# Second attention layer: the softmax bound moved from a selector matmul into free rows of the queries

## The chip, the cores and the metric
The kernel runs on one core of a Trainium2 chip. The metric is the device time of one execution in microseconds; lower is better. Engines: TensorE (PE, with its weight loads shown as PEld), VectorE (DVE), ScalarE (ACT), GpSimd (POOL) and SyncE (SP), which issues the DMAs here.

## What is computed
`x` is 32 images of 16 x 16 tokens with 256 channels. Each of two layers normalizes (group norm) and adds an attention of 16 heads of 16 channels. The first layer is windowed cosine attention. The second, which the change touches, attends over all 256 tokens of an image, heads 0 to 7 looking back and heads 8 to 15 looking ahead:

```python
def _masked_attention(xf, Wq, Wk, Wv, lookahead):
    q, k, v = (jnp.einsum('bnd,hed->bhne', xf, W) for W in (Wq, Wk, Wv))
    s = jnp.einsum('bhqe,bhke->bhqk', q, k) * scale
    mask = i[:, None] <= i[None, :] if lookahead else i[:, None] >= i[None, :]
    s = jnp.where(mask, s, jnp.finfo(s.dtype).min)
    return jnp.einsum('bhqk,bhke->bhqe', jax.nn.softmax(s, axis=-1), v)
```

The heads are concatenated, multiplied by `Wo` and added to the layer's input. (The snippet shortens the reference's three projections to one line.)

## The kernel before
Layer 1 of the code (`layer1`) is the second layer. An image has two channel tiles `o` of 128 channels, 8 heads each: tile 0 looks back, tile 1 ahead. A tile has four row groups `r` of 32 partitions (`own_rows(r)`), each with two heads `e` of 16 channels. A head can't be addressed alone, as a matmul takes 32 rows, so the queries are kept twice, `qm[k][:, o, e, :]`: multiplied by `own`, which is 1/4 in the rows of head `e` and 0 in those of the other head. The keys `kt` are kept once, with both heads. Scores with `qm` are therefore those of one head.

The softmax needs the maximum of each query. The kernel computes the scores twice: once with queries on partitions and masked (`bound_queries` L1011 in fp32, `mask_bounds` L1022, which adds a triangle by a bf16 matmul with the identity), from which VectorE takes the maximum (`take_max` L1165) into `cm`; and once with keys on partitions (`weigh_keys` L979), one 512-column matmul for both heads. From those the maximum is taken away on TensorE: `cm` is transposed (`turn_c` L1080), ScalarE copies it negated into bf16 `ct` (`copy_c` L1140), and `lower_by_bound` L994 adds it by bf16 matmuls with the selector `pick`. ScalarE then takes the exponential (`exponent` L1113) into `weights`, GpSimd zeroes the masked part of the diagonal blocks (`mask` L1219), and TensorE multiplies with the values (`weigh` L1042), ones beside the values giving the sums.

The work of an image is cut into six bursts: WHOLE_0 and WHOLE_0B (tile 0, two row groups each, blocks with all queries), HALVES and HALVES_B (both tiles, the other blocks, 128 columns), WHOLE_1 and WHOLE_1B (tile 1). A burst weighs two row groups of image s (PSUM banks 0, 1 of `G`) while it bounds the other two of image s+1 (banks 2, 3). Below, W0, W0B, H, HB, W1, W1B stand for the bursts and R(burst) for its maximum on VectorE.

`pipeline` runs the stages of every engine in an order written out by hand, each with a lag: lag 1 means that in step s the stage works on image s+1. TensorE's order before is W0, q/k projection of tile 1 (L1056), W0B, turn_c(1), weigh(1) of image s-1, H, value projection (L1068), HB, q/k projection of tile 0, W1, output projection of image s-2 (L1090), W1B, turn_c(0), weigh(0). ScalarE copies the weighed values out (`copy_outputs` L1127, into `ots`), queries and keys of tile 0 (L1120, L1122) and the values (L1134). VectorE copies queries and keys of tile 1 (L1171, L1173), takes four reciprocals of the sums (L1184), normalizes (L1195), divides (L1189) and adds the residual (L1178). SP regroups `ots` through DRAM in eight stores (L947), once both tiles' outputs are copied, fetches them when all eight have landed (L955) and stores results (L961). The next copy into `ots` waits for the eight stores.

Waits are semaphore counts: a burst's bounds wait for `max_done` of the burst before, its weights for `exp_done`; HALVES also wait for `qk_out[1]` and `c_out[1]`, WHOLE_0 for `qk_out[0]` and `c_out[0]`. `A[0]`, `A[1]`, `A[2]` and `E` are further PSUM tiles of 512 columns. `stack` holds queries and keys of two images.

Of the kernel before, what the change touches and what calls it, by code (L numbers as in the profile page):

```python
# [23 lines left out]
BF16 = mybir.dt.bfloat16  # L24
I32 = mybir.dt.int32
ALU = mybir.AluOpType
# [33 lines left out]
class Image:  # L60
# [6 lines left out]
    def plus(self, n):  # L67
        return Image(self.pair, self.offset + n)

# [738 lines left out]
def layer1(nc, ctx, images, out, given, scratch, X, stats2, probs, xh, stack, ident, gavg, A, G, E):  # L808
# [13 lines left out]
    ct = [sb(f"ct1{o}", [P, TOKENS], BF16) for o in range(CT)]  # L822
# [5 lines left out]
    own = sb("own", [P, 2])  # L828
    at_row = sb("at_row", [P, 2])
    pick = sb("pick", [P, 2, P], BF16)  # L830
    n_stat = images * CT
    weights = probs[1]

    flat = [stack[k][:, :, :, :].rearrange("p z h t -> p (z h t)").bitcast(F32) for k in range(2)]
    qm = [flat[k][:, 0:CT * 2 * TOKENS].rearrange("p (o e t) -> p o e t", o=CT, e=2) for k in range(2)]
    kt = [flat[k][:, CT * 2 * TOKENS:CT * 3 * TOKENS].rearrange("p (o t) -> p o t", o=CT) for k in range(2)]
# [14 lines left out]
    with nc.Block() as block:  # L851
# [7 lines left out]
        def _(dve):  # L859
# [7 lines left out]
            slots = ident[:, :].rearrange("p (r x) -> p x r", x=COL)  # L867
            nc.vector.reduce_sum(own[:, :], parity, AX_XY).then_inc(made, 1)
            nc.vector.reduce_sum(at_row[:, :], slots[:, 0:2, :], AX_X).then_inc(made, 1)
            dve.wait_ge(made, 2)  # L870
            nc.vector.tensor_scalar(own[:, :], own[:, :], DIM ** -0.5, None, ALU.mult).then_inc(made, 1)
            nc.vector.tensor_copy(pick[:, :, :], at_row[:, :].unsqueeze(2).to_broadcast([P, 2, P])).then_inc(made, 1)
# [55 lines left out]
    QK_OPS = (3, 2)  # L928
# [7 lines left out]
    with nc.Block() as block:  # L936
# [33 lines left out]
        def _(pe):  # L970
            def weigh_keys(i, b):

                if b is HALVES:
                    wait(pe, qk_out[1], i.count(QK_OPS[1]))
                wait(pe, exp_done, i.count(ALL, b.at) if b.at else i.plus(-1).count(ALL))
                for o in b.tiles:
                    for bank, r in enumerate(b.weigh_rows):
                        at = bank * 512 + b.column(o, 0)
                        nc.tensor.matmul(G[:, at:at + 2 * b.size].rearrange("p (e q) -> p e q", e=2),  # L979
                                         kt[i.k][own_rows(r), o, b.keys_of(o) * P:(b.keys_of(o) + 1) * P],  # L980
                                         qm[i.k][own_rows(r), o, :, b.queries(o)], start=(o == b.tiles[0]), stop=False,
                                         skip_group_check=True)

            def lower_by_bound(i, b):

                if b is WHOLE_0:
                    wait(pe, c_out[0], i.count(1))
                if b is HALVES:
                    wait(pe, c_out[1], i.count(1))
                for o in b.tiles:  # L990
                    for e in range(2):
                        for bank, r in enumerate(b.weigh_rows):
                            at = bank * 512 + b.column(o, e)
                            last = nc.tensor.matmul(G[:, at:at + b.size], pick[own_rows(r), e, :],  # L994
                                                    ct[o][own_rows(r), b.queries(o)], start=False, stop=True,
                                                    skip_group_check=True)
                            if e == 1 and o == b.tiles[-1]:
                                last.then_inc(s_ready, 1)

            def bound_queries(i, b):  # L1000

                if b is WHOLE_0:
                    wait(pe, qk_out[0], i.count(QK_OPS[0]))
                if b is HALVES:
                    wait(pe, qk_out[1], i.count(QK_OPS[1]))
# [42 lines left out]
            def project_qk(i, o):  # L1048

                wait(pe, xh_done, i.count(CT))  # L1050
                if o == 0:
                    wait(pe, ot_out[1], i.plus(-3).count(1))
# [236 lines left out]
```

## Time and profile before

| | us |
|---|---|
| median of 3 runs | 1286.02 (1282.92 to 1295.72) |
| profiled execution | 1287.98 |
| its span | 1286.3 |
| TensorE busy in the span | 1194.4 (93%) |
| VectorE busy | 897.7 (70%) |
| ScalarE busy | 610.9 (47%) |
| GpSimd busy | 207.4 (16%) |
| VectorE copy of k, L1173, mean | 0.415 |
| ScalarE copy of outputs, L1127, mean | 0.597 |
| fetch, L955, issue to landing, median | 2.9 |

The first layer ends near 575 us, the second fills the rest. Times in rows are microseconds from the span's start. PE is the matmul's streaming and PEld its weight load; the two overlap, and matmuls on different row groups overlap too, so the distance from one stage's first load to the next stage's first load is the way to read a stage's length. An fp32 matmul appears as two pairs of load and matmul.

### The profile page before, as it was taken

To read this page: it belongs to the slowest core of one execution; us is meant where nothing else is said; L and a number is where in the kernel's file an instruction comes from. 1 tells how busy PE (TensorE), PEld (TensorE's weight loads), DVE (VectorE), ACT (ScalarE), POOL (GpSimd) and SP (SyncE) were. 2 spreads that over 40 slices of the span, in tenths; PEclk is the share of its full clock that TensorE was granted. 3 is DMA by queue.
4 is the path that set the end of the run, shared out by engine and by line. 5 is a ranking of instruction groups with operands and counts; after the bars stand their busy time and mean duration, and the time that the engine had idled before them with its cause. 6 is when DMAs were issued, how large, how long until landed. Compare 5 with 4: busy or idle time off the path is not lost.

```text
span 1286.3 us, 50697 instructions
## 1 busy us (share of the span) xinstructions
PE 1194.4 (93%) x21404; PEld 864.1 (67%) x21404; DVE 897.7 (70%) x1591; ACT 610.9 (47%) x1019; POOL 207.4 (16%) x271
## 2 busy tenths in 40 slices
PE   6789999999999999958999999999999999999983
PEld 2567777777677677736677776767777777767652
DVE  1488898798888888645576666767666666767643
ACT  2355565555555555512444444444444444445430
POOL 0001111111111111121222212212222212222120
PEclk9699999999999999989999999999999999999987
DMA  2000000000000000010232423333232323333233
GB/s 80 13 20 20 20 17 17 20 16 25 12 24 16 18 12 3 5 38 1 34 65 64 79 48 74 52 70 57 65 58 66 75 51 76 51 71 56 67 58 74
DMA packets 304632, 54.35 MB, mean 42 GB/s; under 512 B 270724, under 2 KB 303766, under 8 KB 304534
## 3 DMA queue, kind: packets, MB, share of 16 engines
q1 hardware_dynamic: 303480, 52.75, 19.9%
q8 instruction: 83, 1.36, 0.4%
q10 hardware_dynamic: 1056, 0.13, 0.1%
q14 instruction: 13, 0.11, 0.0%
HBM read 27.56 MB, written 25.17 MB: 41 GB/s over the span
## 4 chain that ended last, share of the span: by engine, by line
PE 45%; DVE 5%; issue 3%; ACT 1%; DMA 1%; SPq 0%; POOL 0%; POOLq 0%; DVEq 0%
PE psG L979 8%; PE psA L1042 7%; PE psG L1011 6%; PE psA L1056 5%; PE psG L1022 5%; PE psE L1090 5%; PE psA L1068 4%; DVE of L1189 3%; PE psG L994 2%; DVE sums L1184 2%; PE psE L1080 1%; ACT probs L1113 0%; SPq L947 0%; DVE cm L1165 0%; DMA scratch_heads<-ots 0%
## 5 line engine op out<-in xcount | busy, mean ns | idle before, releaser
L1165 DVE TENSOR_REDUCE cm<-psG 128x4 f32<-128x1024 f32 (+1 forms) x192 | 235.2, 1225 | 174.5 <-PE psG L1022 174.3
L1113 ACT ACTIVATE probs<-psG 128x1024 f32<-128x1024 f32 x192 | 196.5, 1023 | 240.5 <-PE psG L994 240.5
L1219 POOL TENSOR_SCALAR_AFFINE_SELECT probs<-probs 128x1024 f32<-128x1024 f32 x128 | 139.1, 1098 | 551.0 <-ACT probs L1113 551.0
L979 PE MATMUL psG<-stack 32*128 32x512 f32 (+1 forms) x1024 | 219.2, 525 | 6.3 <-ACT probs L1113 6.3
L1011 PE MATMUL psG<-stack 32*128 32x256 f32 (+1 forms) x2048 | 219.2, 341 | 4.1 <-DVE cm L1165 2.7
L1011 PEld LDWEIGHTS psG<-stack 32*128 32x128 f32 x2048 | 149.6, 185 | 10.8 <-DVE cm L1165 3.4
L764 POOL TENSOR_TENSOR X<-X,probs 128x96 f32 (+5 forms) x128 | 62.0, 515 | 499.2 <-ACT probs L529 499.2
L443 PE MATMUL psA<-probs,xh 128*128 128x512 f32 x256 | 130.5, 637 | 9.3 <-ACT xh L562 5.3
L1056 PE MATMUL psA<-xh,wqk 128*128 128x256 f32 x512 | 122.6, 383 | 5.7 <-DVE xh L1195 5.7
L979 PEld LDWEIGHTS psG<-stack 32*128 32x128 f32 x1024 | 82.8, 185 | 61.6 <-issue 54.3
L1184 DVE RECIPROCAL sums<-sums 128x128 f32<-128x128 f32 x128 | 115.7, 929 | 12.0 <-DMA sums<-scratch_heads 12.0
L1056 PEld LDWEIGHTS psA<-xh,wqk 128*128 128x128 f32 x512 | 93.3, 192 | 17.4 <-DVE xh L1195 6.4
L1042 PE MATMUL psA<-probs,va 128*32 128x256 f32 (+1 forms) x2048 | 97.8, 332 | 0.9 <-POOL probs L1219 0.9
L522 ACT ACTIVATE probs<-psG 128x1024 f32<-128x1024 f32 x64 | 62.0, 1021 | 76.1 <-PE psG L346 76.1
L634 DVE TENSOR_TENSOR probs<-probs,ebias 128x1024 f32<-128x1024 f32 x64 | 77.9, 1219 | 14.6 <-ACT probs L522 14.5
L1090 PE MATMUL psE<-of,wo 128*128 128x256 f32 x256 | 67.0, 407 | 21.7 <-DVE of L1189 20.5
L707 DVE TENSOR_REDUCE cm<-psG 128x16 f32<-128x1024 f32 x64 | 75.4, 1219 | 14.8 <-PE psG L370 13.9
L1042 PEld LDWEIGHTS psA<-probs,va 128*32 128x32 f32 x2048 | 57.8, 110 | 34.5 <-issue 11.7
L506 ACT ACTIVATE probs<-psA 128x512 f32<-128x512 f32 x64 | 38.2, 597 | 87.1 <-PE psA L443 83.0
L443 PEld LDWEIGHTS psA<-probs,xh 128*128 128x128 f32 x256 | 45.6, 198 | 45.6 <-issue 33.2
L994 PE MATMUL psG<-ct,pick 32*128 32x256 bf16 (+1 forms) x1024 | 74.4, 242 | 0.0
L1090 PEld LDWEIGHTS psE<-of,wo 128*128 128x128 f32 x256 | 48.2, 198 | 36.2 <-DVE of L1189 23.2
(132 smaller groups left out, 1925.5 us busy)
## 6 DMA issues: line engine op xcount, KB each, us to landing
scratch_heads<-ots SPq DMA_DIRECT2D x256, 64.0 KB, 3.6
X<-in_xr SPq DMA_DIRECT2D x32, 256.0 KB, 2.8
raw<-scratch_heads SPq DMA_DIRECT2D x32, 256.0 KB, 2.7
sums<-scratch_heads SPq DMA_DIRECT2D x32, 256.0 KB, 3.0
out<-X SPq DMA_DIRECT2D x32, 256.0 KB, 2.9
probs<-in_wqk SPq DMA_DIRECT2D x1, 512.0 KB, 4.0
wv<-in_wv SPq DMA_DIRECT2D x2, 256.0 KB, 4.2
wqk<-in_wqk SPq DMA_DIRECT2D x1, 512.0 KB, 4.0
```

Source lines behind the costliest of these rows:

```text
L443: last = nc.tensor.matmul(A[t][:], xh[i.k][:, c, t * P:(t + 1) * P], wqk[:, c, :], start=(c == 0), stop=(c == CT - 1))
L634: nc.vector.tensor_tensor(both, both, bias.unsqueeze(2).to_broadcast([P, 4, WINDOWS, WTOK]), ALU.mult).then_inc(biased, 1)
L979: nc.tensor.matmul(G[:, at:at + 2 * b.size].rearrange("p (e q) -> p e q", e=2), kt[i.k][own_rows(r), o, b.keys_of(o) * P:(b.keys_of(o) + 1 ...
L994: last = nc.tensor.matmul(G[:, at:at + b.size], pick[own_rows(r), e, :], ct[o][own_rows(r), b.queries(o)], start=False, stop=True, skip_gr ...
L1011: nc.tensor.matmul(G[:, at:at + b.size], qm[i.k][own_rows(r), o, e, b.queries_of(o) * P:(b.queries_of(o) + 1) * P], kt[i.k][own_rows(r), o ...
L1042: last = nc.tensor.matmul(A[0 if o else 2][COL * c:COL * (c + 1), to:to + b.size], va[i.k][:, b.keys_of(o), TILE_HEADS * o + 2 * r + e, :] ...
L1056: last = nc.tensor.matmul(A[o][:, n * TOKENS:(n + 1) * TOKENS], wqk[:, c, n * CH + o * P:n * CH + (o + 1) * P], xh[i.k][:, c, :], start=(c ...
L1090: last = nc.tensor.matmul(E[:, o * TOKENS:(o + 1) * TOKENS], wo[:, f, o * P:(o + 1) * P], of[:, f, :], start=(f == 0), stop=(f == CT - 1))
L1113: nc.scalar.activation(weights[:, b.weights_at:b.weights_at + 1024], G[:, 0:1024], ACT.Exp).then_inc(exp_done, 1)
L1165: nc.vector.reduce_max(slots, scores, AX_X).then_inc(max_done, 1)
L1184: nc.vector.reciprocal(piece, piece).then_inc(r_done, 1)
L1219: nc.gpsimd.affine_select(out=diagonal, in_=diagonal, compare_op=ALU.is_ge, fill=0.0, base=0, pattern=[[0, QUADS], [0, 2], [sign, P]], cha ...
```

## The change
The bound is no longer added by matmuls of its own. The masked queries of head `e` have 16 rows that are zero, those of the other head. The transposed bound of head `e` is now laid there: `take_max` writes it to the first channel of the other head's rows (the bounds' bank column is `1 - e`), and VectorE adds the negated, transposed `cm` to `qm` in place (`fold_bound`, two `scalar_tensor_tensor` for each tile, masked by `lift`). The keys are kept per head, `km[k][:, o, e, :]`: masked by `own`, with a row of ones (`at_row` as the bias of a ScalarE `Identity`) that meets the bound. One fp32 matmul then gives scores less bound. So `lower_by_bound`, `pick`, `ct` and `copy_c` go; each 512-column weighing matmul becomes two of 256 columns (256 becomes two of 128), with a key tile of its own; the four groups' matmuls are interleaved; all k copies go to ScalarE (four for an image) and only the q copy of tile 1 stays on VectorE. `weights` uses both `probs` buffers in turn. The orders change: turn_c(1) moves ahead of the q/k projection of tile 1, the value projection ahead of H, weigh(1) behind H, and turn_c(0), now into `A[1]`, ahead of the output projection.

```diff
-            def weigh_keys(i, b): ...
-            def lower_by_bound(i, b): ...
-            def bound_queries(i, b): ...
+            def burst(j, b):
+                i = j.plus(-1)
+                weighs, bounds = i.exists(), j.among(images)
+                if weighs:
+                    if b is WHOLE_0:
+                        wait(pe, c_out[0], i.count(FOLDS))
+                    wait(pe, exp_done, i.count(ALL, b.at) if b.at else i.plus(-1).count(ALL))
+                if bounds:
+                    if b is WHOLE_0:
+                        wait(pe, qk_out[0], j.count(QK_OPS[0]))
+                    wait(pe, max_done, j.count(ALL, b.at) if b.at else j.plus(-1).count(ALL))
                 for o in b.tiles:
+                    if b is HALVES and o == 1:
+                        if weighs:
+                            wait(pe, c_out[1], i.count(FOLDS))
+                        if bounds:
+                            wait(pe, qk_out[1], j.count(QK_OPS[1]))
                     for e in range(2):
                         for bank, r in enumerate(b.weigh_rows):
+                            if weighs:
+                                at = bank * 512 + b.column(o, e)
+                                last = nc.tensor.matmul(G[:, at:at + b.size],
+                                                        km[i.k][own_rows(r), o, e, b.keys_of(o) * P:(b.keys_of(o) + 1) * P],
+                                                        qm[i.k][own_rows(r), o, e, b.queries(o)],
+                                                        start=(e == 0 and o == b.tiles[0]), stop=True, skip_group_check=True)
                         for bank, r in enumerate(b.bound_rows):
+                            if bounds:
+                                at = (2 + bank) * 512 + b.column(o, 1 - e)
+                                nc.tensor.matmul(G[:, at:at + b.size],
+                                                 qm[j.k][own_rows(r), o, e, b.queries_of(o) * P:(b.queries_of(o) + 1) * P],
+                                                 km[j.k][own_rows(r), o, e, b.keys(o)],
+                                                 start=(e == 0 and o == b.tiles[0]), stop=False, skip_group_check=True)
+                if bounds:
+                    mask_bounds(b)
...
+            pipeline(pe, images, [B(WHOLE_0), (lambda i: turn_c(i, 1), 0), (lambda i: project_qk(i, 1), 1),
+                                  B(WHOLE_0B), (project_v, 1),
+                                  B(HALVES), (lambda i: weigh(i, 1), -1),
+                                  B(HALVES_B), (lambda i: project_qk(i, 0), 2),
+                                  B(WHOLE_1), (lambda i: turn_c(i, 0), 1), (output, -2),
+                                  B(WHOLE_1B), (lambda i: weigh(i, 0), 0)], LAGS)
...
+            def copy_k(i, o):
+                if o:
+                    wait(act, qk_out[1], i.count(QK_OPS[1], 1))
+                for e in range(2):
+                    nc.scalar.activation(km[i.k][:, o, e, :], A[o][:, TOKENS:2 * TOKENS], ACT.Identity,
+                                         bias=at_row[:, 1 - e:2 - e], scale=own[:, e:e + 1]).then_inc(qk_out[o], 1)
...
+            pipeline(act, images, [(lambda i: copy_outputs(i, 0), -1), X_(WHOLE_0), (lambda i: copy_k(i, 1), 1), X_(WHOLE_0B),
+                                   X_(HALVES), (lambda i: copy_outputs(i, 1), -1), (copy_v, 1), X_(HALVES_B), (copy_q, 2),
+                                   X_(WHOLE_1), (lambda i: copy_k(i, 0), 2), X_(WHOLE_1B)], LAGS)
...
+            def fold_bound(i, o):
+                wait(dve, c_turned[o], i.count(1))
+                for e in range(2):
+                    q = qm[i.k][:, o, e, :]
+                    nc.vector.scalar_tensor_tensor(out=q, in0=(E if o else A[1])[:, 0:TOKENS], scalar=lift[:, 1 - e:2 - e], in1=q,
+                                                   op0=ALU.mult, op1=ALU.add).then_inc(c_out[o], 1)
...
+            pipeline(dve, images, [R(WHOLE_0), (lambda i: fold_bound(i, 1), 0), (copy_q, 1), R(WHOLE_0B), I_(0), (normalize, 2),
+                                   R(HALVES), I_(1), I_(2), R(HALVES_B), I_(3), (divide, -2), R(WHOLE_1),
+                                   (lambda i: fold_bound(i, 0), 1), (residual, -2), R(WHOLE_1B)], LAGS)
```

## Rows read from the trace of the kernel before

**Rows 1.** Busy time by stretch: stretch, its length, each engine's busy us (instructions), clock, DMA.
```profile
800.00:960.00 160.00, 158.63 (x1906) 114.27 (x1900) 109.40 (x125) 73.81 (x108) 33.97 (x32) 1.00 0.32 62
```

**Rows 2.** Loads of the output projection, 640 to 1240 us: durations, first and last start.
```profile
L1090 PEld LDWEIGHTS psE<-of,wo x232: 186/190/191, 650.7 to 1232.1; 128*128 128x128 f32 x116
```

**Rows 3.** Chain of waits, 912 to 925 us: start, length, what.
```profile
916.58 0.04 DVE cm L1165
...
917.72 0.95 DVE sums L1184
...
918.70 1.22 DVE of L1189
...
919.96 1.99 PE psE L1090 x8
```

**Rows 4.** Timeline of weight loads, whole bursts: start, length, instruction, [idle before <-releaser].
```profile
904.49 0.19 PEld L979 LDWEIGHTS psG<-stack 32*128 32x128 f32 x2 [0.20 <-issue]
904.51 0.19 PEld L1011 LDWEIGHTS psG<-stack 32*128 32x128 f32 x2
904.60 0.19 PEld L979 LDWEIGHTS psG<-stack 32*128 32x128 f32 x2
...
905.46 0.10 PEld L994 LDWEIGHTS psG<-ct,pick 32*128 32x128 bf16 x2 [0.22 <-issue]
905.77 0.11 PEld L1022 LDWEIGHTS psG<-above,identb 128*128 128x128 bf16 x2 [0.21 <-issue]
905.90 1.60 PEld L1056 LDWEIGHTS psA<-xh,wqk 128*128 128x128 f32 x8
907.82 0.19 PEld L979 LDWEIGHTS psG<-stack 32*128 32x128 f32 x2 [0.33 <-issue]
...
909.23 0.25 PEld L1080 LDWEIGHTS psE<-ident,cm 128*128 128x128 f32 x2
909.64 1.24 PEld L1042 LDWEIGHTS psA<-probs,va 128*32 128x32 f32 x32 [0.17 <-issue]
```

**Rows 5.** The same timeline, the burst of halves that follows.
```profile
911.08 0.19 PEld L979 LDWEIGHTS psG<-stack 32*128 32x128 f32 x2 [0.20 <-issue]
...
912.37 0.10 PEld L1022 LDWEIGHTS psG<-above,identb 128*128 128x128 bf16 x1
...
912.71 1.60 PEld L1068 LDWEIGHTS psA<-wv,xh 128*128 128x128 f32 x8
```

**Rows 6.** The same view where the pipeline fills: bursts that only bound.
```profile
581.20 0.73 PEld L1011 LDWEIGHTS psG<-stack 32*128 32x128 f32 x8 [0.33 <-DVE cm L1165]
582.26 0.11 PEld L1022 LDWEIGHTS psG<-above,identb 128*128 128x128 bf16 x2 [0.33 <-issue]
...
587.42 0.97 PEld L1011 LDWEIGHTS psG<-stack 32*128 32x128 f32 x16 [0.33 <-DVE cm L1165]
588.51 0.10 PEld L1022 LDWEIGHTS psG<-above,identb 128*128 128x128 bf16 x1
```

**Rows 7.** Timeline of VectorE in the same step.
```profile
906.20 1.23 DVE L1165 TENSOR_REDUCE cm<-psG 128x4 f32<-128x1024 f32 x1 [2.03 <-PE psG L1022]
908.02 0.69 DVE L1171 TENSOR_TENSOR stack<-psA,own 128x512 f32<-128x512 f32 x1 [0.59 <-PE psA L1056]
...
913.02 1.23 DVE L1165 TENSOR_REDUCE cm<-psG 128x8 f32<-128x1024 f32 x1 [0.85 <-PE psG L1022]
```

**Rows 8.** Groups by line and form, ScalarE: busy us, mean ns, idle before.
```profile
L1113 ACT ACTIVATE probs<-psG 128x1024 f32<-128x1024 f32 x192 | 196.5, 1023 | 240.5 <-PE psG L994 240.5
...
L1120 ACT ACTIVATE stack<-psA,own 128x256 f32<-128x256 f32 x64 | 26.8, 470 | 53.4 <-PE psA L1056 53.4
...
L1122 ACT ACTIVATE stack<-psA 128x256 f32<-128x256 f32 x32 | 12.3, 383 | 0.0
```

**Rows 9.** Timeline of SP's DMA issues.
```profile
911.95 7.11 SPq L947 DMA_DIRECT2D scratch_heads<-ots  x8
921.99 0.37 SPq L955 DMA_DIRECT2D raw<-scratch_heads  x1
```

More of the change, by code:

```diff
@@ L68, in plus, with exists @@
         return Image(self.pair, self.offset + n)
+    def exists(self):
+        return not isinstance(self.pair, int) or self.pair * 2 + self.offset >= 0
     def among(self, images):
@@ L970, in _ @@
         def _(pe):
[L971 to L975, printed above, removed]
-                for o in b.tiles:
[L977 to L982, printed above, removed]
@@ L1000, in bound_queries @@
[L1000 to L1005, printed above, removed]
-                wait(pe, max_done, i.count(ALL, b.at) if b.at else i.plus(-1).count(ALL))
-                for o in b.tiles:
-                    for e in range(2):
-                        for bank, r in enumerate(b.bound_rows):
-                            at = (2 + bank) * 512 + b.column(o, e)
-                            nc.tensor.matmul(G[:, at:at + b.size],
-                                             qm[i.k][own_rows(r), o, e, b.queries_of(o) * P:(b.queries_of(o) + 1) * P],
-                                             kt[i.k][own_rows(r), o, b.keys(o)], start=(e == 0 and o == b.tiles[0]), stop=False,
-                                             skip_group_check=True)
@@ L1043, in weigh @@
                                                     va[i.k][:, b.keys_of(o), TILE_HEADS * o + 2 * r + e, :],
-                                                    weights[:, at:at + b.size], start=b.whole, stop=not b.whole,
+                                                    weights[i.k][:, at:at + b.size], start=b.whole, stop=not b.whole,
                                                     tile_position=(0, COL * c), skip_group_check=True)
@@ L1052, in project_qk @@
                     wait(pe, ot_out[1], i.plus(-3).count(1))
+                else:
+                    wait(pe, c_out[0], i.plus(-1).count(FOLDS))
                 wait(pe, qk_out[o], i.plus(-1).count(QK_OPS[o]))
@@ L1086, in output @@
                 if i.plus(2).among(images):
-                    wait(pe, c_out[1], i.plus(2).count(1))
+                    wait(pe, c_out[1], i.plus(2).count(FOLDS))
                 for o in range(CT):
@@ L1094, in B @@
             def B(b):
[L1095 to L1103 removed]
+                return lambda j: burst(j, b), 1, 1
+            pipeline(pe, images, [B(WHOLE_0), (lambda i: turn_c(i, 1), 0), (lambda i: project_qk(i, 1), 1),
[4 more added lines that the diff above has]
+                                  B(WHOLE_1B), (lambda i: weigh(i, 0), 0)], LAGS)
         @block.scalar
```

82 lines of the change are left out of this document (27 added, 55 removed).

## The prediction
> **What bounds the kernel now.** I read the busy time by stretch first, then one step's weight loads in order of time, then the chain of waits, and last VectorE, ScalarE and the DMA queue in the same step. Between 800 and 960 us TensorE is busy for 158.63 of 160 us at a granted clock of 1.00 [rows 1]; VectorE is at 68% and ScalarE at 46%. So the second layer is TensorE's, and a step (one image) costs what its stages cost in TensorE's order. The output projection recurs 29 times between 650.7 and 1232.1 us; the last start belongs to the eighth load of its group, 1.44 us after the first, so the step is (1232.1 - 1.4 - 650.7)/28 = 20.71 us [rows 2].
>
> From load to load, a whole burst takes 1.41 us (904.49 to 905.90, again 907.82 to 909.23), a projection 1.92, a transposition of the bounds 0.41 (909.23 to 909.64), the weighing of values 1.44 (909.64 to 911.08) [rows 4, 5], a burst of halves 1.63 (911.08 to 912.71) [rows 5]. A step holds 4 x 1.41 + 2 x 1.63 + 2 x 0.41 + 2 x 1.44 + 4 x 1.92 (q/k twice, v, output) = 20.28 us. One wait is left: the output projection waits 0.37 us for the division, which stands in the chain behind R(HALVES_B), the fourth reciprocal and the product: 916.58 to 919.96, 3.38 us [rows 3]. Sum 20.65 against 20.71 for the mean step; I carry the 0.06 along.
>
> **The change, part by part.**
>
> *Selectors go.* In a whole burst the fp32 scores start at 904.49 and the mask's load at 905.77: 1.28 us, with the last L994 load at 905.46 in between [rows 4]. What a burst is without L994 the trace shows itself, where the pipeline fills and only bounds are computed: 581.20 to 582.26, 1.06 us; halves 587.42 to 588.51, 1.09 us, against 911.08 to 912.37, 1.29 [rows 5, 6]. These bursts have the same bound matmuls; the row groups of the weights run beside them. So L994 costs 0.22 per whole burst (I use 0.21, as all these times are rounded) and 0.20 per burst of halves, not the 0.31 that its own slot (905.46 to 905.77) suggests: part of that is the gap before a load over all rows, which stays. Saved: 4 x 0.21 + 2 x 0.20 = 1.24 us a step. PE work falls to 19.04 us, a whole burst to 1.20, halves to 1.43.
>
> *Keys per head.* Each weighing matmul of 512 columns becomes two of 256 (halves: 256 becomes 2 x 128). Columns are the same, but 4 (halves: 8) load-and-matmul pairs are added, as many as L994 gives up. Each of the four row groups then carries what a bound group carries today, and the bound groups set the length today. What can break this is only what the groups share. In the first two rounds of a whole burst four fp32 loads start within 0.02 us (904.49, 904.51) and the next round 0.11 later (904.60): 27 ns a pair [rows 4]. Halves need four pairs per 0.11 us throughout. Lower end: nothing. Upper end: 68 ns a pair, the slowest a burst shows (16 pairs in 1.09 us [rows 6]), although those pairs wait for their own group's stream. I take nothing, since the two full rounds are the nearest rows.
> The Trainium skill ("TensorE: Matmul & The Clock Gate", Back-to-back issue gap) gives about 81 ns for each pair of load and matmul at 128 columns in a real kernel, which would speak against this change. Today's halves contradict it for row groups: 24 fp32 and 8 L994 pairs stand in 1.29 us, 40 ns each [rows 5].
>
> *Bursts wait once, at their start.* Today only the bound half waits for the maximum. Now the weights, issued first, wait too. R starts 1.71 us after a whole burst (904.49 to 906.20), 1.94 after halves (911.08 to 913.02) [rows 4, 5, 7]; with L994 gone 1.50 and 1.74. It takes 1.23, and TensorE follows about 0.05 later (918.70 + 1.22 to 919.96 [rows 3]). So the next burst can't start before 2.78 (after halves 3.02) us. Two neighbours are close: W1B and W0 with only weigh(0) between, 1.20 + 1.44 = 2.64: wait 0.14; and H and HB with only weigh(1) between now, 1.43 + 1.44 = 2.87: wait 0.15.
>
> *The division.* H starts at 6.65 in the new order (W0 at 0; turn 1.20; q/k 1.61; W0B 3.53; v 4.73). R(H) runs 8.39 to 9.62, HB starts at 9.67, R(HB) at 11.41 (R(H) and two reciprocals before it take at most 916.58 to 918.70 plus 0.95, 3.07 us [rows 3], and end within 0.05 of that), and 3.38 later, 14.79, the output may start. TensorE is there at 14.63 (q/k 11.10, W1 13.02, turn 14.22): wait 0.16 instead of 0.37. W1B 16.71, weigh 17.91, then W0 at 19.49 with its wait. Step: 19.04 + 0.14 + 0.15 + 0.16 = 19.49, plus the 0.06: 19.55.
>
> *Folds on VectorE, k copies off it.* Two folds of 256 elements for each tile half. No row has this operation; above it lies a product of 512 from PSUM (0.69), below it half of that, 0.35, if nothing of it is fixed [rows 7]. I take 0.43, near the lower end and the plain copy of 256 in the table, since it too makes one pass over 256 elements: 0.86 a pair, 1.72 a step, less the copy of k, 0.42: VectorE rises by 1.3 us. fold(1) stands between R(W0) (ends 2.73) and copy_q, whose projection ends at 3.53 and reaches VectorE 0.2 later (905.90 to 908.02 is 2.12 [rows 4, 7]): it ends at 3.59, cover 0.14 us. fold(0) stands after R(W1), with 1 us to spare before R(W1B). At 0.69 each, copy_q starts 0.4 late.
>
> *k copies on ScalarE.* Four with a pointer scale and a pointer bias. A copy takes 383 ns, with a pointer scale 470 [rows 8]; a second pointer at the same price gives about 560, at no price 470. A pair is 1.0 us. ScalarE gains 4 x 0.56 and loses 0.38 + 2 x 0.38: about 1.1 us on some 9.9 a step. The one that can hurt is copy_k(1), in front of exp(W0B): copy_q 3.73 to 4.42, copy_k to 5.5, exp (1.02 [rows 8]) to 6.45; H needs it at 6.65. Cover 0.15. Without that cover each late us is a late us of the step; with slow folds (0.4 late) 0.25.
>
> *Later regroup.* weigh(1) moves behind HALVES, so ots is full later: weigh(1) ends at 9.52 (9.67 with the wait that follows it, no matter), its copy of 0.60 (table) is done about 0.74 later, 10.26, SP issues at about 10.4. Eight stores and their landing take 10.04 us (911.95 to the fetch at 921.99 [rows 9]): 20.43, which is 0.94 us into the next step. Behind that wait, on ScalarE, stands the first copy of outputs, and behind it exp(W0), which W0B needs at 3.53. Copy 0.94 to 1.54, exp to 2.57: cover 0.9 us. The fetch, queued behind it on SP, lands some 3 us later (table), near 4.5, before the first reciprocal at 6.2.
>
> *Two weight buffers.* exp no longer waits for the weighing of the image before, which allows the moves above; no wait of that kind ends last today. Nothing.
>
> **The sum.** 20.71 - 19.55 = 1.16 us a step. Steps with all six bursts full: 31 of the 32 images (the last has no next image's bounds): 36.0 us. The last image's six bursts without bounds lie in a serial chain with exp and gain 0.21 each, 1.3. Fill and the last two outputs, which wait for DMA, keep their length. Profiled execution: span 1286.3, time 1288.0; 1288.0 - 37.3 = 1250.7. The median of the runs shown is 2.0 lower, so 1249.
>
> **Rivals.**
> 1. *Halves don't get shorter.* If pairs there cost 40 ns as in today's halves [rows 5], 32 pairs take 1.28 instead of about 1.09, and the 0.20 isn't won: 2 x 0.2 x 31 = 12 us, 1261. For it: the spacing of today's bursts fits. Against it: their bound groups run at their own stream's pace. The same order of loss follows from slow folds or copies (0.25 x 31 = 8, 1257).
> 2. *Slower: pairs are issue- or load-bound in halves.* Place: 32 loads and 32 matmuls of 128 columns. At 68 ns a pair the burst lasts 2.18 instead of 1.09: +2.2 a step, 1249 + 68 = 1317. The gain is gone at 53 ns, slower by 1% from 59 ns. Against it: the two rounds at 27 ns.
> By the skill's 81 ns ("TensorE: Matmul & The Clock Gate", Back-to-back issue gap) it would be 2.6 us, or 1342.
> 3. *The stores become the ring.* copy_outputs(1), stores, copy_outputs(0), exp(W0), W0B, v, H, weigh(1) form a ring with 0.9 us of slack. Each us beyond it lengthens every step by one: stores of 12 us give about 1280, from 12.5 us it is slower. For it: they start later than today in the step. Against it: they meet no more traffic than today, since fetch and store of the image still fall outside them.
> 4. *The change takes L994 away but TensorE waits the same time.* The mask's load then comes 0.2 after the bounds as now: 1286. Against it: the filling bursts [rows 6], which have exactly this sequence.
>
> **How the numbers follow.** Forecast, 1240 to 1258: 0.58. Rival 1 and its like, 1258 to 1270: 0.16. Better than 1240, if the three waits also go (0.45 x 31 = 14, 1235): 0.05. Rivals 3 (part) and 4, 1273 to 1299: 0.12. Slower (2, 3): 0.09. A measurement of this kernel tells about 1% (13 us) from no change. Faster by over 1%, below 1273: 0.80; within 1%: 0.11; slower: 0.09. Range 1238 to 1270.
>
> **What would show it.** Right: no L994, output projections 19.5 to 19.6 us apart, whole bursts 1.20 and halves 1.43 from load to next stage, waits of 0.1 to 0.2 us for VectorE's maximum before HALVES_B and WHOLE_0, folds near 0.43 us. Wrong: halves longer than 1.6 us (1, 2); ScalarE's copy of outputs waiting past 1.8 us into the step (3); TensorE waiting for exp before HALVES (copy_k chain); mask loads 1.28 after the burst's start (4).

## The result

| | before | after |
|---|---|---|
| median | 1284.47 us (1277.4 to 1295.72, 4 runs) | 1248.04 us (1242.07 to 1257.64, 4 runs) |
| ratio | 1 | 0.9729 (0.9668 to 0.9791) |
| span of the profiled execution | 1286.3 | 1244.4 |
| step of the second layer | 20.71 | 19.45 |

Forecast were 1249 us and a step of 19.55. The step first: these are the loads of the output projection in the changed kernel (durations, first and last start; L1089 here, [rows 2] before):

```profile
L1089 PEld LDWEIGHTS psE<-of,wo x232: 186/190/191, 646.0 to 1192.1; 128*128 128x128 f32 x116
```

The step is (1192.1 - 1.4 - 646.0)/28 = 19.45 us. TensorE is busy for 159.41 of 160 us at a granted clock of 1.00, where it was 158.63 [rows 1]; VectorE went from 109.4 to 129.4, ScalarE from 73.8 to 86.0:

```profile
800.00:960.00 160.00, 159.41 (x1996) 114.88 (x1996) 129.44 (x158) 85.99 (x125) 35.84 (x34) 1.00 0.36 67
```

Timeline of the weight loads of one step after (start, length, instruction, idle before; L998 weighs, L1007 bounds, L1020 masks), to be held against [rows 4, 5]:

```profile
882.48 0.11 PEld L1020 LDWEIGHTS psG<-below,identb 128*128 128x128 bf16 x2 [0.33 <-issue]
882.81 1.24 PEld L1040 LDWEIGHTS psA<-probs,va 128*32 128x32 f32 x32 [0.21 <-issue]
884.25 0.19 PEld L998 LDWEIGHTS psG<-stack 32*128 32x128 f32 x2 [0.20 <-DVE cm L1165]
...
885.32 0.11 PEld L1020 LDWEIGHTS psG<-above,identb 128*128 128x128 bf16 x2 [0.33 <-issue]
885.45 0.25 PEld L1079 LDWEIGHTS psE<-ident,cm 128*128 128x128 f32 x2
885.67 1.60 PEld L1056 LDWEIGHTS psA<-xh,wqk 128*128 128x128 f32 x8
887.59 0.19 PEld L998 LDWEIGHTS psG<-stack 32*128 32x128 f32 x2 [0.33 <-issue]
...
890.72 0.19 PEld L998 LDWEIGHTS psG<-stack 32*128 32x128 f32 x2 [0.33 <-DVE cm L1165]
890.74 0.19 PEld L1007 LDWEIGHTS psG<-stack 32*128 32x128 f32 x2
890.83 0.19 PEld L998 LDWEIGHTS psG<-stack 32*128 32x128 f32 x2
...
891.83 0.10 PEld L1020 LDWEIGHTS psG<-above,identb 128*128 128x128 bf16 x1
...
892.37 1.24 PEld L1040 LDWEIGHTS psA<-probs,va 128*32 128x32 f32 x32 [0.21 <-issue]
893.81 0.19 PEld L998 LDWEIGHTS psG<-stack 32*128 32x128 f32 x2 [0.20 <-DVE cm L1165]
...
898.39 0.25 PEld L1079 LDWEIGHTS psA<-ident,cm 128*128 128x128 f32 x2
898.94 1.59 PEld L1089 LDWEIGHTS psE<-of,wo 128*128 128x128 f32 x8 [0.30 <-DVE of L1196]
```

A whole burst takes 1.20 us (884.25 to 885.45) instead of 1.41. In halves the mask comes 1.11 us after the start (890.72 to 891.83) instead of 1.29, and rounds of four pairs follow 0.11 us apart. One wait is left, before the output projection, 0.33 us: the transposition takes 0.22 from 898.39, so TensorE is free at 898.61 and starts at 898.94.

Where the 41.9 us between the two profiled spans lie, from the first load of the second layer's first projection (573.5 before, 561.8 after) and the groups of output projections: first layer, untouched by the change, -11.7; fill of the second layer up to its first output projection 77.2 and 84.2, +7.0; 28 steps at -1.26, -35.3; the last three outputs -1.9. The second layer by itself gained 30.2 us. The first part is scatter: over the profiled kernels of this study, which share this first layer, the second layer began between 557.3 and 576.7 us (579.6 in the last one below, which adds matmuls between the layers). The scatter goes together with the clock: in the four profiles in which the second layer began by 562.4 us, the granted clock stayed at 1.00 from 100 to 540 us; in each of the other eight it fell to 0.50 there once or twice, for 3.4 us each, in the kernel before once (length, PE, PEld, DVE, ACT, POOL, clock, DMA):

```profile
231.60:235.00 3.40, 3.40 (x32) 3.07 (x29) 2.44 (x4) 2.10 (x3) 0.00 (x0) 0.50 0.00 0
```

TensorE had been waiting before the clock fell (from 225.0 to 231.6 us it was busy for 4.67 of 6.60 us; in the changed kernel for 6.50), and if half the clock costs half of the time, 3.4 us of it are worth 1.7 of the 11.7: the clock is a small part of it. Why TensorE waited there in some executions stays open. Medians therefore need the interval beside them. The mean step is the sharper measure: the three profiles with the order recip_early below give 19.16, 19.12 and 19.16 us.

VectorE and ScalarE around the same step (start, length; [rows 7] are those of before):

```profile
886.90 0.87 DVE L1179 SCALAR_TENSOR_TENSOR stack<-psE,lift,stack 128x256 f32<-128x256 f32 x2
...
895.56 1.23 DVE L1165 TENSOR_REDUCE cm<-psG 128x8 f32<-128x1024 f32 x1 [0.19 <-PE psG L1020]
896.71 0.94 DVE L1191 RECIPROCAL sums<-sums 128x128 f32<-128x128 f32 x1
897.68 1.20 DVE L1196 TENSOR_TENSOR of<-raw,sums 128x512 f32<-128x512 f32 x1
```

```profile
885.09 0.60 ACT L1131 ACTIVATE ots<-psA 128x512 f32<-128x512 f32 x1 [1.45 <-DMA scratch_heads<-ots]
885.59 1.02 ACT L1111 ACTIVATE probs<-psG 128x1024 f32<-128x1024 f32 x1
888.52 1.02 ACT L1125 ACTIVATE stack<-psA,at_row,own 128x256 f32<-128x256 f32 x2 [1.92 <-DVE stack L1171]
889.43 1.02 ACT L1111 ACTIVATE probs<-psG 128x1024 f32<-128x1024 f32 x1
```

The pair of folds takes 0.87 us, the pair of k copies 1.02. exp(W0B) ends at 890.45 (889.43 + 1.02), 0.27 before H starts. The copy of outputs now waits for the stores until 885.09, 0.84 us into the step.

### The profile page after: what moved, and what is told of

Its sections match the earlier page's. It is cut to its first block, busy times and chain, and to the rows that moved or that the text cites. A ratio compares the mean times of both kernels' runs of the same rounds, so it can differ in the third digit from the quotient of the medians.

```text
span 1244.4 us, 50834 instructions
## 1 busy us (share of the span) xinstructions
PE 1161.2 (93%) x21404; PEld 844.7 (68%) x21404; DVE 944.2 (76%) x1687; ACT 636.4 (51%) x1051; POOL 209.5 (17%) x271
## 4 chain that ended last, share of the span: by engine, by line
PE 42%; DVE 5%; issue 3%; SPq 2%; DMA 2%; ACT 1%; DVEq 0%; ACTq 0%
PE psG L998 13%; PE psA L1040 7%; PE psA L1056 5%; PE psG L1020 5%; PE psE L1089 5%; PE psA L1068 4%; DVE of L1196 3%; DVE sums L1191 2%; SPq L952 2%; PE psG L1007 2%; DMA scratch_heads<-ots 1%; DVE cm L1165 1%; PE psE L1079 1%; ACT probs L1111 0%; DMA sums<-scratch_heads 0%
## 5 line engine op out<-in xcount | busy, mean ns | idle before, releaser
L998 PE MATMUL psG<-stack 32*128 32x256 f32 (+1 forms) x2048 | 221.7, 344 | 11.1 <-DVE cm L1165 6.6
L1007 PE MATMUL psG<-stack 32*128 32x256 f32 (+1 forms) x2048 | 222.4, 345 | 4.3 <-DVE cm L1165 2.4
L998 PEld LDWEIGHTS psG<-stack 32*128 32x128 f32 x2048 | 151.8, 187 | 69.5 <-DVE cm L1165 27.5
L1007 PEld LDWEIGHTS psG<-stack 32*128 32x128 f32 x2048 | 151.3, 187 | 7.4 <-DVE cm L1165 3.3
L1056 PE MATMUL psA<-xh,wqk 128*128 128x256 f32 x512 | 126.4, 392 | 5.6 <-DVE xh L1202 5.6
L1056 PEld LDWEIGHTS psA<-xh,wqk 128*128 128x128 f32 x512 | 95.9, 198 | 17.9 <-DVE xh L1202 6.3
L1125 ACT ACTIVATE stack<-psA,at_row,own 128x256 f32<-128x256 f32 x128 | 65.1, 561 | 59.3 <-DVE stack L1171 59.3
L638 DVE TENSOR_TENSOR probs<-probs,ebias 128x1024 f32<-128x1024 f32 x64 | 77.9, 1220 | 11.4 <-ACT probs L526 11.3
L1089 PE MATMUL psE<-of,wo 128*128 128x256 f32 x256 | 69.0, 416 | 17.5 <-DVE of L1196 15.8
L1131 ACT ACTIVATE ots<-psA 128x512 f32<-128x512 f32 x64 | 38.2, 597 | 84.3 <-DMA scratch_heads<-ots 52.9
```

Source lines behind the costliest of these rows:

```text
L638: nc.vector.tensor_tensor(both, both, bias.unsqueeze(2).to_broadcast([P, 4, WINDOWS, WTOK]), ALU.mult).then_inc(biased, 1)
L998: last = nc.tensor.matmul(G[:, at:at + b.size], km[i.k][own_rows(r), o, e, b.keys_of(o) * P:(b.keys_of(o) + 1) * P], qm[i.k][own_rows(r), ...
L1007: nc.tensor.matmul(G[:, at:at + b.size], qm[j.k][own_rows(r), o, e, b.queries_of(o) * P:(b.queries_of(o) + 1) * P], km[j.k][own_rows(r), o ...
L1056: last = nc.tensor.matmul(A[o][:, n * TOKENS:(n + 1) * TOKENS], wqk[:, c, n * CH + o * P:n * CH + (o + 1) * P], xh[i.k][:, c, :], start=(c ...
L1089: last = nc.tensor.matmul(E[:, o * TOKENS:(o + 1) * TOKENS], wo[:, f, o * P:(o + 1) * P], of[:, f, :], start=(f == 0), stop=(f == CT - 1))
```

## The experiments

Where steps are compared, they come from the output projection's starts in each kernel's profile, as above.

**Selectors back.** Ahead of the mask, each burst again adds bf16 matmuls with a selector, both operands zero. The signal that the scores are complete moves behind them:

```diff
+                for o in b.tiles:
+                    for e in range(2):
+                        for bank, r in enumerate(b.weigh_rows):
+                            if weighs:
+                                at = bank * 512 + b.column(o, e)
+                                last = nc.tensor.matmul(G[:, at:at + b.size], sel0[own_rows(r), e, :],
+                                                        ct0[own_rows(r), b.queries(o)], start=False, stop=True,
...
                 if bounds:
                     mask_bounds(b)
```

> The changed kernel with the selector matmuls put back behind each burst's fp32 matmuls, with zeros in selector and bounds, so that they add nothing and everything else stays. Theory (the selectors' place on TensorE is what was won, 0.21 us per whole burst and 0.20 per burst of halves): TensorE's work in a step grows by 1.24 us; the wait for the division shrinks from 0.33 to about 0.12, since TensorE comes there 0.41 later and the maximum of HALVES_B only 0.20 later. Step 19.45 to about 20.5 us, 31 steps: about 1280 us. Rival (order and second buffer made the gain): step below 19.7 us, about 1250.

Measured: 1275.61 us, ratio to before 0.9976 (0.9957 to 0.9996); step 20.49, expected 20.5. Its weight loads (L1002 weighs, L1018 selects, L1032 masks):

```profile
915.98 0.19 PEld L1002 LDWEIGHTS psG<-stack 32*128 32x128 f32 x2 [0.20 <-DVE cm L1177]
...
916.73 0.32 PEld L1018 LDWEIGHTS psG<-ct,sel 32*128 32x128 bf16 x4
917.26 0.11 PEld L1032 LDWEIGHTS psG<-above,identb 128*128 128x128 bf16 x2 [0.21 <-issue]
```

From the start to the mask 1.28 us, exactly as before the change, against 1.07 without (884.25 to 885.32). The price of the selectors is shown, and so is the 0.21 instead of the 0.31 of their own slot. The new order and the folds, with the selectors kept, gain little over the kernel before: 20.49 against 20.71 us a step.

**Old order.** No selectors, but the stages of TensorE, ScalarE and VectorE in the order of before. The folds follow the maxima, and ScalarE keeps the copies of k where the change put them. TensorE's part of the edit:

```diff
-            pipeline(pe, images, [B(WHOLE_0), (lambda i: turn_c(i, 1), 0), (lambda i: project_qk(i, 1), 1), ...
+            pipeline(pe, images, [B(WHOLE_0), (lambda i: project_qk(i, 1), 1),
+                                  B(WHOLE_0B), (lambda i: turn_c(i, 1), 0), (lambda i: weigh(i, 1), -1),
+                                  B(HALVES), (project_v, 1),
+                                  B(HALVES_B), (lambda i: project_qk(i, 0), 2),
+                                  B(WHOLE_1), (output, -2),
+                                  B(WHOLE_1B), (lambda i: turn_c(i, 0), 1), (lambda i: weigh(i, 0), 0)], LAGS)
...
```

> The changed kernel with the stage orders of the kernel before: turn_c(1) behind WHOLE_0B, weigh(1) ahead of HALVES, turn_c(0) behind WHOLE_1B, the folds behind the maxima they follow; no selectors, both weight buffers kept. Theory (the order is what hides the folds): WHOLE_0 must wait for the fold, 1.50 + 1.23 + 0.86 = 3.6 us after the start of WHOLE_1B, where TensorE is there after 1.20 + 0.41 + 1.44 = 3.05: wait 0.55; the output projection waits 0.56 instead of 0.33, as no transposition stands ahead of it. Step about 20.3 us, about 1273. Rival (selectors alone count, the order is neutral): 19.4 to 19.6 us, about 1248. The fill, in which the changed kernel took some 9 us longer up to its first output projection, tells whether that comes from the order (then it is shorter here) or from the longer chain of each image.

Measured: 1277.04 us, ratio 1.0002 (0.9972 to 1.0032), step 20.53 where 20.3 were expected; the total is not distinguishable from before. Who waited in the steady part (total us, times, longest):

```profile
PE psG L998 <- DVE stack L1179: 17.2, 26, 0.7
PEld psE L1089 <- DVE of L1196: 14.7, 26, 0.6
```

That is 0.66 us a step for the fold, where 0.55 were expected, and 0.57 for the division. A third piece was not foreseen: HALVES takes 1.59 us from load to next stage instead of HALVES_B's 1.44 (911.40 to 912.99), because its tile 1 waits for the folds of that tile. They end at 911.86, and the loads of tile 1 begin 0.25 us after the last round of tile 0 (911.73, 911.98), where rounds otherwise follow 0.11 apart.

Together 0.66 + (0.57 - 0.33) + 0.15 = 1.05 of the 1.08 us by which this step is longer than 19.45. So the selectors' 1.24 us are mostly given back if the folds aren't hidden, and the moved stages gain little if the selectors stay. The gain needs both. The fill, up to the first output projection, took 80.3 us; more on that below.

**One buffer of weights.**

```diff
-    weights = probs
+    weights = [probs[1], probs[1]]
...
-                    wait(act, pv_done[1], i.plus(-2).count(1))
+                    wait(act, pv_done[1], i.plus(-1).count(1))
```

The wait at the start of WHOLE_0, on `pv_done[0]`, changes in the same way.

> The changed kernel with one buffer of weights; exp(HALVES) then has to wait until weigh(1) of the image before has read them. Theory (the buffer is worth nothing by itself, but the new place of weigh(1) needs it): exp(HALVES) starts 2.0 us later, right behind weigh(1), and HALVES_B waits about 1.2 us for it: step about 20.65 us, about 1285. Rival (the second buffer does nothing): 19.45 us, 1248.

Measured: 1283.67 us, ratio 1.0044 (1.0022 to 1.0066), step 20.80 against 20.65 expected. The wait is where it was expected, exp behind weigh(1) and the burst behind exp (timelines of ScalarE and of the weight loads):

```profile
901.38 1.02 ACT L1111 ACTIVATE probs<-psG 128x1024 f32<-128x1024 f32 x1 [3.54 <-PE psA L1040]
```

```profile
902.52 0.19 PEld L998 LDWEIGHTS psG<-stack 32*128 32x128 f32 x2 [1.54 <-issue]
```

The burst starts 0.12 us after exp's end (902.40), not 0.05 as I had assumed; that is half of the miss. So with weigh(1) behind H the second buffer is worth 1.35 us a step. That it would buy nothing in the old order was not run; in the trace of before, exp never waits for the weighing of values.

**Reciprocals early.** Only VectorE's order changes:

```diff
-            pipeline(dve, images, [R(WHOLE_0), (lambda i: fold_bound(i, 1), 0), (copy_q, 1), R(WHOLE_0B), I_(0), (normalize, 2),
-                                   R(HALVES), I_(1), I_(2), R(HALVES_B), I_(3), (divide, -2), R(WHOLE_1),
+            pipeline(dve, images, [(normalize, 2), R(WHOLE_0), (lambda i: fold_bound(i, 1), 0), (copy_q, 1), R(WHOLE_0B), I_(0), I_(1),
+                                   R(HALVES), I_(2), I_(3), R(HALVES_B), (divide, -2), R(WHOLE_1),
...
```

> The changed kernel with VectorE's order alone changed: normalize ahead of the maximum of WHOLE_0, reciprocals 0 and 1 ahead of that of HALVES, 2 and 3 ahead of that of HALVES_B, so that only the product stands between that maximum and the output projection. Theory (the 0.33 us of waiting left in each step is the chain maximum, fourth reciprocal, product): the wait goes and nothing takes its place; step 19.12 us, 10 us less, about 1238. Rival (VectorE at about 80% has no room, the maxima come late and the bursts wait for them): step 19.4 us or more, 1247 or more.

Measured: 1232.22 us, ratio to before 0.9642 (0.9615 to 0.9668); step 19.16, expected 19.12. In its step this version beats both kernels. In its trace the product follows the maximum at once, and TensorE waits for nothing before L1089:

```profile
890.31 1.23 DVE L1165 TENSOR_REDUCE cm<-psG 128x8 f32<-128x1024 f32 x1 [0.19 <-PE psG L1020]
891.45 1.13 DVE L1196 TENSOR_TENSOR of<-raw,sums 128x512 f32<-128x512 f32 x1
```

```profile
893.13 0.25 PEld L1079 LDWEIGHTS psA<-ident,cm 128*128 128x128 f32 x2
893.35 1.60 PEld L1089 LDWEIGHTS psE<-of,wo 128*128 128x128 f32 x8
```

On another chip:

> The kernel recip_early again, as the base for the run that follows: step 19.1 to 19.2 us, 9 to 11 us faster than the changed kernel.

Measured: 1250.85 us, ratio 0.9729 (0.966 to 0.9798), step 19.12. The step repeats, the total scatters from 1231.66 to 1255.06, so on this chip the total's ratio is no better than the changed kernel's 0.9729; the step alone shows the gain of 0.3 us.

**The same order in the kernel before.**

> The kernel before, with VectorE's order alone changed as in recip_early: normalize first, reciprocals 0 and 1 ahead of the maximum of HALVES, 2 and 3 ahead of that of HALVES_B. Theory (the wait for the division is its own chain in both kernels and independent of the selectors): TensorE's 0.36 to 0.5 us of waiting go, step 20.71 to about 20.3 us, 13 us less than before. Rival (the gain of recip_early hangs on the new stage order): 20.6 us or more.

Measured: 1282.71 us, ratio 0.9944 (0.9898 to 0.9989), step 20.27 against 20.71. The expected 20.3 came; the total is 7 us lower than before's where 13 were expected, and the fill of this profile is 4.8 us longer (82.0 against 77.2, see below). The division's wait is a chain of its own in both kernels. Between the two kernels with this order of VectorE the change is worth 1.11 to 1.15 us a step (20.27 against 19.16 and 19.12).

**Stores held back.** Two runs in which SP waits longer before it issues the eight stores:

```diff
                 wait_alone(sp, ot_out[1], i.count(1))
+                if i.plus(3).among(images):
+                    wait_alone(sp, proj_qk[0], i.plus(3).count(1))
```

> The changed kernel, with SP holding the stores of the outputs back until the q/k projection of tile 0 in the same step is done, 2.7 us later than now. Theory (stores, copy of outputs, exp(WHOLE_0), WHOLE_0B and the stages up to that projection form a ring, which now has about 0.95 us of slack): from the start of WHOLE_0B to the end of that projection 9.6 us, 0.2 to the issue, 9.7 for stores and landing, 0.6 to the start of exp, 1.0 for exp, 0.05: step 21.0 to 21.1 us, about 1.6 longer, 49 us in all. Rival (the transfers are hidden, the fetch lands later and nobody waits): 19.45 us, no change.

Measured: 1346.05 us, ratio 1.0443 (1.0347 to 1.0539); the mean step is 22.58. The ring, a chain of waits that closes on itself from step to step, exists: copy of outputs behind the stores, exp behind the copy, WHOLE_0B behind exp. Timelines of ScalarE and of the weight loads:

```profile
913.52 0.60 ACT L1133 ACTIVATE ots<-psA 128x512 f32<-128x512 f32 x1 [4.23 <-DMA scratch_heads<-ots]
914.01 1.02 ACT L1113 ACTIVATE probs<-psG 128x1024 f32<-128x1024 f32 x1
```

```profile
915.15 0.19 PEld L1000 LDWEIGHTS psG<-stack 32*128 32x128 f32 x2 [2.24 <-issue]
```

Of the 28 steps 11 take 21.1 to 21.9 us, near the expected length. The other 17 take 23.0 to 24.0 us, and there the granted clock falls. Busy time by stretch (stretch, length, PE, PEld, DVE, ACT, POOL, clock, DMA):

```profile
892.80:896.20 3.40, 3.40 (x20) 2.23 (x13) 1.99 (x2) 1.16 (x2) 1.10 (x1) 0.51 0.43 149
896.20:916.70 20.50, 18.58 (x242) 13.19 (x241) 13.33 (x19) 9.70 (x15) 3.25 (x3) 1.00 0.31 54
916.70:920.10 3.40, 3.40 (x12) 2.30 (x14) 2.60 (x4) 0.69 (x1) 1.10 (x1) 0.50 0.17 58
```

In these 28 steps there are 17 stretches of 3.4 us at 1.2 GHz instead of 2.4. The one at 916.70 starts 1.5 us after the end of TensorE's wait of some 1.9 us before WHOLE_0B (a load gap of 2.24, of which 0.33 stand between these stages anyway). The changed kernel has no such stretch between 595 and 1199 us. The value projection that lies in one takes 3.40 us (916.36 to 919.76 in the loads) instead of 1.92.

The smaller delay lets SP wait only for the bounds of HALVES_B (`max_ready`):

> The changed kernel, with SP holding the stores back until TensorE has finished the bounds of HALVES_B in the same step, some 0.8 to 0.9 us later than now. Theory (the ring through the stores has 0.95 us of slack, and beyond it each us costs one and more): still inside; ScalarE copies the first outputs 0.8 us later, exp(WHOLE_0) with it, and TensorE doesn't wait: step 19.45 to 19.55 us. Rival (the ring already bounds the step, any delay counts): 20.2 us or more.

Measured: 1272.63 us, ratio 0.9843 (0.9751 to 0.9935), mean step 19.88, single ones from 19.46 to 20.56. Both sides missed. The stores start 1.95 us after HALVES_B starts (894.14, 896.09) instead of 0.87 (893.81, 894.68), a delay of 1.08 rather than the 0.8 to 0.9 I had worked out. From issue to fetch they take anything from 9.5 to 10.9 us over the steps of both kernels. So the slack of 0.95 us, worked out with one duration, is about used up at a delay of 1.1. The granted clock stayed at 1.00 over these 28 steps.

**Slow copies of k.** A third copy of 256 elements on ScalarE, into a spare tile, ahead of copy_k(1):

```diff
+                    nc.scalar.activation(spare[:, :], A[o][:, TOKENS:2 * TOKENS], ACT.Identity,
+                                         bias=at_row[:, 1:2], scale=own[:, 0:1]).then_inc(spare_done, 1)
                 for e in range(2):
```

> The changed kernel with a third, useless copy of 256 elements ahead of the two copies of k of tile 1 on ScalarE. Theory (the copies stand in front of exp(WHOLE_0B), which ends 0.27 us before HALVES starts): 0.46 us more ScalarE time, of which about 0.22 are covered; step 19.45 to about 19.7 us, 7 us in all. Rival (ScalarE at half its time has room for it anywhere): 19.45 us, no change.

Measured: 1269.68 us, ratio 0.985 (0.9775 to 0.9924); step 19.80, so 0.34 longer for 0.46 us of work. exp(W0B) ends at 907.34 and HALVES starts 0.12 later:

```profile
906.31 1.03 ACT L1113 ACTIVATE probs<-psG 128x1024 f32<-128x1024 f32 x1
```

```profile
905.23 1.60 PEld L1070 LDWEIGHTS psA<-wv,xh 128*128 128x128 f32 x8
907.46 0.19 PEld L1000 LDWEIGHTS psG<-stack 32*128 32x128 f32 x2 [0.64 <-DVE cm L1170]
```

The cover was 0.12 to 0.15 us, as the prediction had it (0.15), not the 0.22 of the expectation. ScalarE is at half its time, and still not free at this place.

**Fill with a warm clock.** recip_early with 20 useless matmuls in TensorE's idle time between the layers:

```diff
+            for n in range(8):
+                nc.tensor.matmul(A[0][:, 0:P], ident[:, :], ident[:, :], start=True, stop=True)
             pe.wait_ge(sum_in, 1)
...
+            for n in range(12):
+                nc.tensor.matmul(A[0][:, 0:P], ident[:, :], ident[:, :], start=True, stop=True)
```

> recip_early with 20 useless fp32 matmuls of 128 columns into a free bank, 8 ahead of the group norm's matmul between the layers and 12 behind it, where TensorE idles for some 4.5 and 5.6 us. Theory (the fill of the second layer is long, 80 to 86 us to the first output projection where the kernel before took 77, because TensorE ran up to 23 us of it at the granted clock 0.50, after its idle time between the layers): TensorE stays at 1.00 at the start of the fill, which takes about 77 us; 3 to 4 us faster than recip_early. Rival (the fill is bound by the longer chain of one image, copy of q, copies of k, maximum, fold): no change.

Measured: 1248.91 us, ratio 0.9688 (0.9619 to 0.9756), beside recip_early's 0.9729 on that chip: the totals don't tell them apart. The fill does. Busy time from the first q/k projection to the first output projection, first the kernel before, then the changed one, recip_early on the same chip, and warm (the clock is the third figure from the right):

```profile
573.50:650.70 77.20, 70.80 (x738) 50.68 (x738) 39.05 (x43) 28.75 (x46) 11.94 (x11) 0.98 0.13 20
```

```profile
561.80:646.00 84.20, 74.12 (x740) 52.61 (x740) 42.90 (x52) 32.84 (x51) 12.09 (x11) 0.86 0.10 16
```

```profile
557.30:639.70 82.40, 72.17 (x740) 51.62 (x740) 42.05 (x51) 32.61 (x51) 12.29 (x11) 0.89 0.10 16
```

```profile
579.60:658.00 78.40, 68.28 (x739) 49.01 (x740) 42.07 (x51) 32.61 (x51) 12.27 (x11) 0.93 0.10 17
```

With the idle time between the layers filled, the clock over the fill is 0.93 instead of 0.89, and the fill 4.0 us shorter. The first profile of recip_early lies between, with 0.92 and 81.2 us:

```profile
562.40:643.60 81.20, 70.98 (x740) 51.53 (x741) 42.04 (x51) 32.62 (x51) 12.29 (x11) 0.92 0.10 16
```

So one profile of warm stands against two that differ by 1.2 us: that the matmuls shorten the fill is likely, not shown, and the 77 us of the expectation were not reached.

What the clock costs in the fill can be estimated, though, from how long it was at 0.50 there, if half the clock costs half of that time:

| kernel | fill | of it at clock 0.50 | fill less half of that |
|---|---|---|---|
| before | 77.2 | 2.9 | 75.8 |
| before_recip | 82.0 | 14.9 | 74.6 |
| selectors_back | 85.7 | 19.0 | 76.2 |
| old_order | 80.3 | 11.3 | 74.7 |
| changed kernel | 84.2 | 22.9 | 72.7 |
| recip_early | 81.2 | 13.3 | 74.6 |
| recip_early_2 | 82.4 | 17.8 | 73.5 |
| warm | 78.4 | 10.2 | 73.3 |

The kernel before has two steps of 20.71 in this stretch and the changed one two of 19.45, so at equal clocks the fill should have been 2.5 us shorter; by the last column it is 3.1 shorter. By this estimate the clock accounts for the 7.0 us by which it was longer, and the longer chain of an image, the rival in the expectation of warm, isn't needed to explain them. before_recip, which has selectors and no folds, has a slow clock as well, so the change need not be what slows it. What makes the clock fall in one kernel's fill and hardly in another's stays open, as I tried nothing inside the fill itself.

## Why the prediction was right

**The selectors' price: right.** 0.21 and 0.20 us, taken from the bursts of the filling pipeline [rows 6], came out as 0.21 (1.28 to 1.07) and 0.18 (1.29 to 1.11), and putting them back gave 20.49 for 20.5.

**Pairs in halves: right.** 32 pairs stand in 1.11 us, 35 ns each, and rounds of four are 0.11 apart, 28 ns each. Rivals 1 and 2 fall, and rival 4 with them, as the mask comes 1.07 us after the start of a whole burst. One sign of rivals 1 and 2 appeared all the same: HALVES takes 1.65 us to its next stage (890.72 to 892.37), over the 1.6 that was named; but its pairs are through as early as those of HALVES_B, which takes 1.44, and the rest is the gap ahead of weigh told of below. The Trainium skill's 81 ns a pair ("TensorE: Matmul & The Clock Gate", Back-to-back issue gap) is not what interleaved row groups take in this trace: 28 to 35 ns.

**Waits for the maximum: the mechanism right, the size wrong.** 0.14 and 0.15 were expected, nothing was measured: W0 follows weigh(0) after the same 0.20 gap as before [rows 4], and the maximum it needs ends at 884.15, in time for 884.25:

```profile
882.92 1.23 DVE L1165 TENSOR_REDUCE cm<-psG 128x4 f32<-128x1024 f32 x1 [0.59 <-PE psG L1020]
```

The step that failed is that the prediction took each stage's length over from the old order. Where weigh follows a mask, its first load now stands 0.33 us behind the mask's (882.48 to 882.81); from a mask to a transposition it was 0.13, in the trace of before:

```profile
909.10 0.11 PEld L1022 LDWEIGHTS psG<-above,identb 128*128 128x128 bf16 x2 [0.21 <-issue]
909.23 0.25 PEld L1080 LDWEIGHTS psE<-ident,cm 128*128 128x128 f32 x2
```

In return the transposition takes 0.22 in front of a projection (885.45 to 885.67) instead of 0.41 in front of weigh [rows 4]. The gap between full-array and column-tiled matmuls didn't go away, it moved from behind the transposition to behind the burst. That fills the time in which the maximum is awaited. TensorE's work is 19.12 us instead of 19.04: two stages grew by 0.20 each, two transpositions shrank by 0.19 each, and the rest is in roundings of the stages.

**The division: right chain, wait mis-sized.** 3.38 us from the maximum to the projection (895.56 to 898.94), to the hundredth. But TensorE arrives 0.19 earlier at it, as its transposition is shorter, so that 0.33 instead of 0.16 us are waited. 19.12 + 0.33 = 19.45: the two errors of the waits, 0.29 too much and 0.17 too little, and the 0.08 of work nearly cancel.

**Folds and copies: right in the main.** 0.43 a fold (0.87 the pair; the mean over the steady part is 0.47) and 0.56 a copy of k (561 ns) were forecast and measured. exp(W0B) ends 0.27 before H; I had 0.20 by the timetable and called 0.15 covered. VectorE's busy time rose by 1.6 us a step, not 1.3. The prediction left out that a normalization would now lie beside GpSimd's mask; the pair of them takes 1.04 us (first two rows, after) instead of 0.64 (last two, before). It ended no wait here:

```profile
890.58 1.10 POOL L1227 TENSOR_SCALAR_AFFINE_SELECT probs<-probs 128x1024 f32<-128x1024 f32 x1 [5.71 <-ACT probs L1111]
891.11 1.04 DVE L1202 TENSOR_SCALAR xh<-X,rs_y,shift 128x256 f32 x2
...
910.39 1.10 POOL L1219 TENSOR_SCALAR_AFFINE_SELECT probs<-probs 128x1024 f32<-128x1024 f32 x1 [5.49 <-ACT probs L1113]
911.53 0.64 DVE L1195 TENSOR_SCALAR xh<-X,rs_y,shift 128x256 f32 x2
```

**The stores: right.** 0.94 us into the step was forecast, 0.84 is in the step shown (0.54 in the next). Rival 3's ring is real, with about the slack that was forecast. Its price, a us for each us beyond the slack, was too low by the clock's part, which no sum of durations holds: 22.58 us a step in late_regroup, against 21.1 to 21.9 where the clock didn't fall.

**The second buffer: right** as a condition, as one_buffer shows; that it is worth nothing alone was not run.

**The sum.** Of the 37.3 us forecast, 32.5 lie in the 28 steps between output projections, which gained 35.3. The other 4.8 (three steps and the last image) were to come in the fill and at the end; the end gained 1.9, and the fill, which was otherwise to keep its length, grew by 7.0: this step failed. The runs show 22.9 us of it at clock 0.50 where the kernel before had 2.9, about 10 us by the estimate above. So the second layer gained 30.2 us, not 37.3, and the profiled execution still came out 41.9 us faster because its first layer, which the change leaves alone, happened to be 11.7 shorter. In the medians, 36.4 us apart, the fill doesn't show by itself, as the first layer alone scatters by some 20 us. That 1249 met 1248 so closely is luck; that the kernel is faster, and by about 1.2 us a step, is not.

## What to carry to other kernels

Price a part that is to be removed from a place in the trace where it is already missing, such as a filling pipeline, and not from its own slot. A removal and the reordering that hides its replacement can each be worth 0.2 us a step and together 1.26: sum the waits of the new order before judging either. After such a change look again at the one chain that still ends last; here the order of four reciprocals gave another 0.3 us a step.

## What the runs showed of the hardware

With waits of some 1.9 us in each step, in a layer where TensorE is otherwise busy, the granted clock fell from 1.00 to 0.50 for 3.4 us 17 times in 28 steps (late_regroup), and so the delay cost more than itself: 22.58 us a step, where steps without such a stretch take 21.1 to 21.9. With the shorter delay of mid_regroup it stayed at 1.00.

Changing the form in which the array is used costs TensorE time that no instruction owns: 0.33 us from a full-array bf16 mask to column-tiled weights (882.48 to 882.81) against 0.13 to another full-array load (885.32 to 885.45). With the order of stages it moved, from behind the transposition to behind the mask, and didn't go.

A burst started 0.12 us after exp's end (one_buffer, slow_k), while the output projection started 0.04 to 0.06 after VectorE's product (918.70 + 1.22 to 919.96 before, 897.68 + 1.20 to 898.94 after).

A VectorE operation grew beside one of GpSimd: a normalization of 256 elements took 314 to 410 ns in the kernel before, where GpSimd's mask never lay beside it. In the changed kernel the 26 that run beside the mask between 660 and 1190 us took 720 ns on average, the other 26 took 400; in recip_early they took 950 and 400.
